# FFN layer pair on one core: first transfer split, thresholds in two steps, and DMA transposes for two operands

## The reference, cut to what matters

```python
x = x + L0_ffn(L0_cond(x, length, conv_w), w_gate, w_up, w_down)
x = x + L1_ffn(L1_cond(x, ...), W_base, ...)        # x: (8, 128, 512)

# L0_cond: y = masked mean of x over its last axis; a 5-tap convolution over the rows; x * sigmoid(.)
# L0_ffn: rows of x rounded to 8-bit integers by their own maximum, weights to -1, 0, 1 by their mean;
#         h = silu(xq @ Wg.T) * (xq @ Wu.T)         # 1376 columns
#         h rounded to integers again, @ Wd.T
# L1_cond: lora_delta = lora_B @ lora_A * 0.5
cb = codebook / max(abs(codebook))
wg = (weight + lora_delta).reshape(512, 4, 128)
normalized = wg / exp(scale_log)
idx = searchsorted((cb[:-1] + cb[1:]) * 0.5, normalized)
w_eff = (cb[idx] * scale).reshape(512, 512) + lora_delta
# x @ w_eff.T, then L1_ffn: x @ W_base.T + b_base + four experts of rank 8 weighted by a softmax
```

## Time and profile before

| | us |
|---|---|
| timed runs | 154.81, 155.97, 156.15 (median 155.97) |
| profiled execution, its own time | 154.66 |
| its span, first to last instruction | 152.9 |
| granted TensorE clock, mean | 1.000 of full speed |

### The profile page before, as it was taken

One profiled execution on the slowest core, in us unless ns is written; L12 is line 12 of the kernel. 1 busy time (PEld: TensorE's weight loads), 2 busy tenths in 40 slices (PEclk: granted clock), 3 DMA queues, 4 the chain that ended last, 5 costly groups with the idle time before them and its releaser, 6 DMA issues.

```text
span 152.9 us, 2333 instructions
## 1 busy us (share of the span) xinstructions
PE 141.7 (93%) x758; PEld 89.2 (58%) x758; DVE 113.8 (74%) x302; ACT 95.8 (63%) x163; POOL 11.0 (7%) x31
## 2 busy tenths in 40 slices
PE   6679999998799959999988999999999999999993
PEld 2256665753356736637636465565576766787792
DVE  2799999989999999999999767979893031035561
ACT  3899998996997966955827479786731403400200
POOL 7000000000000034100005200000000000000000
PEclk9999999999999999999999999999999999999999
DMA  5999999749500000000000000000000000000193
GB/s 166 389 406 417 417 419 399 272 154 392 194 0 0 0 2 4 0 0 0 4 0 0 0 0 6 0 0 2 0 4 0 0 0 0 0 4 0 61 373 115
DMA packets 6687, 16.06 MB, mean 105 GB/s; under 512 B 674, under 2 KB 1058, under 8 KB 6676
## 3 DMA queue, kind: packets, MB, share of 16 engines
q1 hardware_dynamic: 6676, 15.92, 27.5%
HBM read 13.82 MB, written 2.10 MB: 104 GB/s over the span
## 4 chain that ended last, share of the span: by engine, by line
PE 48%; DVE 29%; ACT 10%; issue 8%; DMA 2%; SPq 0%; ACTq 0%
PE bank L924 15%; PE bank L871 9%; ACT tern_d L491 6%; PE bank L837 6%; PE bank L843 6%; DVE hmax L1273 5%; DVE raw_gate L1270 5%; DVE junk L1109 2%; DMA cond<-in_cond_w 2%; DVE rmax L1159 2%; PE bank L882 2%; PE bank L856 2%; ACT cond L457 1%; PE bank L931 1%; DVE tern_i L1154 1%
## 5 line engine op out<-in xcount | busy, mean ns | idle before, releaser
L837 PE MATMUL bank<-tern_g,head_sb 128*128 128x464 bf16 (+1 forms) x96 | 22.5, 357 | 2.0 <-ACT head_sb L528 1.2
L843 PE MATMUL bank<-tern_u,head_sb 128*128 128x464 bf16 (+1 forms) x96 | 22.5, 357 | 0.0
L924 PE MATMUL bank<-m_h,fr 128*128 128x512 f32 (+1 forms) x72 | 22.3, 378 | 0.0
L871 PE MATMUL bank<-tern_d,delta 128*128 128x512 bf16 (+1 forms) x88 | 20.5, 379 | 0.3 <-ACT b_full L666 0.2
L592 ACT ACTIVATE raw_gate<-raw_gate,hq 128x1376 int16<-128x1376 f32 x8 | 11.5, 1440 | 13.0 <-DVE hq L1280 13.0
L1270 DVE TENSOR_TENSOR raw_gate<-bank,wbt 128x464 f32<-128x464 f32 (+1 forms) x24 | 15.1, 631 | 4.5 <-ACT wbt L585 4.4
L585 ACT ACTIVATE wbt<-bank,s_g 128x464 f32<-128x464 f32 (+1 forms) x24 | 15.3, 639 | 1.9 <-PE bank L837 1.9
L1273 DVE TENSOR_REDUCE hmax<-raw_gate 128x1 f32<-128x464 f32 (+1 forms) x24 | 15.1, 630 | 0.8
L750 PE MATMUL bank<-wbt,cond 128*128 128x512 f32 x32 | 14.8, 599 | 0.0
L843 PEld LDWEIGHTS bank<-tern_u,head_sb 128*128 128x128 bf16 x96 | 9.3, 98 | 9.2 <-DVE raw_gate L1270 0.2
L924 PEld LDWEIGHTS bank<-m_h,fr 128*128 128x128 f32 x72 | 13.2, 189 | 2.7
(11 more groups left out here) (174 smaller groups left out, 234.7 us busy)
## 6 DMA issues: line engine op xcount, KB each, us to landing
raw_gate<-in_w_gate_t SPq DMA_DIRECT2D x4, 688.0 KB, 7.6
raw_up<-in_w_up_t SPq DMA_DIRECT2D x4, 688.0 KB, 12.6
xs<-in_x SPq DMA_DIRECT2D x8, 256.0 KB, 13.0
out_x<-xs SPq DMA_DIRECT2D x7, 256.0 KB, 2.2
raw_down<-in_w_down_t SPq DMA_DIRECT2D x2, 768.0 KB, 5.4
cond<-in_cond_w SPq DMA_DIRECT2D x4, 256.0 KB, 4.4
wbt<-in_w_base_t SPq DMA_DIRECT2D x4, 256.0 KB, 9.6
raw_down<-in_w_down_t SPq DMA_DIRECT2D x2, 512.0 KB, 7.6
```

The costliest lines, as they stand in the source:

```text
L837: mm = pe.matmul(bank_g[n % 2][:, 0:w], xq_t[:, b % 2, k, :], tern_g[:, k, f0:f0 + w], start=(k == 0), stop=(k == KH - 1))
L843: mm = pe.matmul(bank_u[n % 2][:, 0:w], xq_t[:, b % 2, k, :], tern_u[:, k, f0:f0 + w], start=(k == 0), stop=(k == KH - 1))
L871: mm = pe.matmul(bank_down[:], h_t[0:rows, b % 2, j, :], tern_d[0:rows, j, :], start=(j == 0), stop=(j == KF - 1))
L924: pe.matmul(bank_y[n_res][:, h0:h1], a[:, b, k, :], m[:, k, h0:h1], start=(n == 0), stop=False)
```

## The change

- The head transfer is split: first the 128 short rows (codebook, lengths, indices, scales; 36 floats each), then LoRA A and B once, as a transfer `lora0` of 64 rows by 1024 floats. The deltas are multiplied from 64 rows, and all four come at the start, after 5 warm-up matmuls instead of 7.
- `scaled_weight(1)` goes from ACT to POOL, as one multiplication of 128x512; `condn_done` becomes one semaphore per quarter, and `normalise(0)` waits slice by slice.
- The thresholds are ordered in two steps: two instructions ahead of `normalise(0)`, four after the second mask.
- Hidden activations 0 to 6 are transposed by one DMA each on SP's queue, from `h_i` (now 1408 columns wide) into one buffer `ht_i`; ACT copies them to `h_t` in two instructions at the end of iteration b+1, right ahead of `hidden_round(b+1)`. Only entry 7 goes through PE.
- Quantised x(3) to x(7) are transposed by DMA on the same queue, two buffers, x(b+3) issued behind h(b). x(0) to x(2) go through PE.
- Order: `x1_transposes(b-3)`, `x1_high` and `x1_low` come after the second chunk, not before it; `fold(3,3)` before `gate_up(0,1)`; m copies in the order 1, 0, 2, 3; `x_max(5, 8)` ahead of `residual(0)`, and the gates and scales of x(5) to x(7) ahead of `x1_low(0)` and `residual(1)`; `conv(2)` right after `gate_up(3,1)`.

```diff
-            sp.dma_start(head_sb[:], head).then_inc(ld_head, 16)
+            sp.dma_start(head_sb[:, 2 * H:HEAD], head).then_inc(ld_head, 16)
+            sp.dma_start(head_sb[0:RANK0, 0:2 * H], lora0).then_inc(ld_lora, 16)
             for k in range(KH):
-                sp.dma_start(cond[:, k, :], cond_v[:, k, :]).then_inc(ld_cond[k], 16)
+                load_cond(k)
...
+            def transpose_x(b):
+                sp.wait_ge(xq_pool_done, b - 1)
+                if b - 2 >= X_BY_DMA:
+                    sp.wait_ge(xt_done, b - 1)
+                sp.dma_start(xt_i[:, b % 2, :, :], xq_bits[:, b % 2, :].bitcast(I16), transpose=True)\
+                    .then_inc(xt_landed[b % 2], 16)
+
+            def transpose_h(b):
+                sp.wait_ge(hint_done, b + 1)
+                if b >= 1:
+                    sp.wait_ge(ht_done, ht_copies(b - 1))
+                sp.dma_start(ht_i, h_i[:, b % 2, :], transpose=True).then_inc(ht_landed, 16)
+
+            for b in range(NB):
+                if b < H_BY_DMA:
+                    transpose_h(b)
+                if X_BY_DMA <= b + 3 < NB:
+                    transpose_x(b + 3)
...
+            for k in SCALED_BY_POOL:
+                pool.wait_ge(inv_done, 1)
+                pool.wait_ge(ld_cond[k], 16)
+                pool.tensor_tensor(cond[:, k, :].rearrange("p (g i) -> p g i", g=KH),
...
-            for n, i in enumerate(T_ORDER):
+            for i in T_ORDER:
                 diagonals(i)
-                if n == 3:
-                    scaled_weight(1)
...
             def hidden_evacuate(b):
+                if b < H_BY_DMA:
+                    act.wait_ge(ht_landed, 16 * (b + 1))
+                    if b >= 2:
+                        act.wait_ge(down_ps, b - 1)
+                    act.activation(h_t[0:FL, b % 2, KW, :], ht_i[0:FL, KW, :], ACT.Copy).then_inc(ht_done, 1)
+                    act.activation(h_t[:, b % 2, 0:KW, :], ht_i[:, 0:KW, :], ACT.Copy).then_inc(ht_done, 1)
+                    return
...
+                if 1 <= b < NB:
+                    hidden_evacuate(b - 1)
                 if b < NB:
                     hidden_round(b)
...
-            pe.wait_ge(ld_head, 16)
-            lora_delta(0)
-            lora_delta(1)
+            pe.wait_ge(ld_lora, 16)
+            for k in range(KH):
+                lora_delta(k)
...
+                gate_up(b, 1)
+                if b == 3:
+                    conv(2)
                 if b >= 4:
                     x1_transposes(b - 3)
-                gate_up(b, 1)
                 if b == 0:
-                    fold(KH - 1, 3)
                     conv(1)
...
-                if b >= 1:
+                if b - 1 >= H_BY_DMA:
                     hidden_transposes(b - 1)
-                if 2 <= b < NB - 1 or b == 0:
+                if b != 1 and b + 1 < X_BY_DMA:
                     x_transposes(b + 1)
...
+            def inner_thresholds():
                 dve.tensor_tensor(t(1), t(1), t(3), ALU.min)
-                link(dve.tensor_tensor(t(5), t(5), t(3), ALU.max))
+                dve.tensor_tensor(t(5), t(5), t(3), ALU.max).then_inc(th_done, 1)
+
+            def outer_thresholds():
+                dve.wait_ge(th_done, 1)
                 dve.tensor_tensor(t(0), t(0), t(1), ALU.min)
...
+            inner_thresholds()
             normalise(0)
-            masks(0, 0, 1)
-            ordered_thresholds()
-            masks(0, 1)
+            masks(0, 0, 2)
+            outer_thresholds()
+            masks(0, 2, 3)
+            dve.wait_ge(th_done, 2)
+            masks(0, 3)
...
                 if b == 3:
+                    x_max(5, NB)
                     residual(0)
+                if b < NB:
+                    hidden_chunk(b, 1)
                 if b >= 4:
                     x1_low(b - 3)
-                if b < NB:
-                    hidden_chunk(b, 1)
...
                 if b == 3:
+                    y_reciprocal(2)
+                    gates(2)
+                    x_scales(5, NB)
                     x1_low(0)
                 if 3 <= b <= NB + 1:
                     residual(b - 2)
```

More of the change, by code:

```diff
@@ L59 @@
 EPS = 1e-5
-WARM_HEAD = 7
+WARM_HEAD = 5
 HALF = TAPS // 2
@@ L63 @@
 GROUPS = [(0, 2), (2, 5), (5, NB)]
-CONV_WITH_XT = {4: 2}
+X_BY_DMA = 3
+H_BY_DMA = 7
+KW = KF - 1
 TINY_SQUARE = 1e-36
 STAND_IN = 1e-15
+SCALED_BY_POOL = (1,)
+M_ORDER = (1, 0, 2, 3)
 T_ORDER = (3, 1, 5, 0, 2, 4, 6)
@@ L75, with build @@
 SUMMED_BY_ACT = 3
-def build(nc, x, head, w_gate_t, w_up_t, w_down_t, cond_w, w_base_t, b_base,
+def build(nc, x, head, lora0, w_gate_t, w_up_t, w_down_t, cond_w, w_base_t, b_base,
           lora1, router, conv_band, out):
@@ L271, in build @@
         delta_ps = sem("delta_ps")
-        condn_done = sem("condn_done")
+        condn_done = [sem(f"condn_done{k}") for k in range(KH)]
         norm_done = sem("norm_done")
@@ L345, in chunk_no, with xt_landings, ht_copies @@
             return NC * b + c
+        def xt_landings(b):
+            return sum(1 for i in range(X_BY_DMA, b + 1) if i % 2 == b % 2)
+        def ht_copies(b):
+            return 2 * min(b + 1, H_BY_DMA) + 3 * max(0, b + 1 - H_BY_DMA)
         block = ctx.enter_context(nc.Block())
@@ L456, in scaled_weight @@
                     c = slice(g * GROUP, (g + 1) * GROUP)
-                    ins = act.activation(cond[:, k, c], cond[:, k, c], ACT.Copy, scale=scl_inv[:, k, g:g + 1])
-                ins.then_inc(condn_done, 1)
+                    act.activation(cond[:, k, c], cond[:, k, c], ACT.Copy,
+                                   scale=scl_inv[:, k, g:g + 1]).then_inc(condn_done[k], 1)
             scaled_weight(0)
@@ L524, in x_evacuate @@
             def x_evacuate(b):
-                act.wait_ge(xt_ps, b + 1)
+                if b < X_BY_DMA:
+                    act.wait_ge(xt_ps, b + 1)
+                    src = bank_xTi[b].rearrange("p (k e) -> p k e", k=KH)
+                else:
+                    act.wait_ge(xt_landed[b % 2], 16 * xt_landings(b))
+                    src = xt_i[:, b % 2, :, :]
                 if b >= 2:
                     act.wait_ge(gu_ps, NC * (b - 1))
-                act.activation(xq_t[:, b % 2, :, :], bank_xTi[b].rearrange("p (k e) -> p k e", k=KH),
-                               ACT.Copy).then_inc(xt_done, 1)
+                act.activation(xq_t[:, b % 2, :, :], src, ACT.Copy).then_inc(xt_done, 1)
             def conv_out(g):
@@ L543, in m_copy @@
                 act.wait_ge(fold_ps, k + 1)
-                if k == 0:
+                if k == M_ORDER[0]:
                     act.wait_ge(tern_out, 2 * NC - 1)
@@ L627, in _ @@
                     silu_chunk(b, 1)
+                if b >= 4:
+                    x1_high(b - 3)
                 if b == 0:
-                    for k in range(KH):
+                    for k in M_ORDER:
                         m_copy(k)
@@ L939, in _ @@
                 gate_up(b, 0)
+                if b == 0:
+                    fold(KH - 1, 3)
                 if b == 1:
@@ L1324, in _ @@
                                       ms_h.bitcast(F32), ALU.subtract).then_inc(msl_done, 1)
-                    x_max(5, NB)
                     y_safe(2)
```

81 lines of the change are left out of this document (44 added, 37 removed).

## The result

The change makes the kernel slightly slower: 157.40 us median (156.58 to 158.03, 10 runs) against 155.95 (154.68 to 156.20, 10 runs) of the kernel before, ratio 1.0115 with a 95% interval of 1.0077 to 1.0154. The forecast was 150.6. The profiled execution has a span of 154.9 us, where before had 152.9.

What follows compares the result with a forecast made beforehand. Bound by hops between engines to about 33 us, DVE to 80.7, then PE; gains of 1.8 us (start) and 2.95 us (loop), together 4.8, took 155.4 to 150.6 us, with an 8-in-10 range of 148.5 to 156.0.

Steps and rivals of the forecast that it cites:

- in the new place PE is idle: Start, PE: two of four deltas leave the place between codebooks 0 and 1, where four took 1.88 us, for idle time.
- The LoRA rows land on 64 partitions at half the rate: Start: the rows land 0.65 us later; with POOL disturbing DVE, the reason for the start gain's lower bound of 1.0 us.
- the 4.65: Start, DVE: `normalise(0)` follows `cond` slice by slice and starts at about 4.65 us instead of 6.26.
- The forecast of 1.8 us for the start: Common gain of the ACT, DVE and PE queues at the start: 1.8 us, bounds 1.0 and 2.2.
- T: Loop: time for a DMA-transposed h to land, taken as 4.5 us, bounds 2.6 and 8.9; up to 4.4 fully hidden.
- x1 transposes 0.44, `down(1)` 2.38: Loop, iteration 3, PE: durations in us summed from 76.75, with two `gate_up` groups of 1.56 each, to 82.7.
- The 0.93 us wait for `residual(1)`: Loop, PE: this wait goes, since the residual is ready at 82.05 and PE arrives at 82.7.
- 1.1 us lost to the later start: Loop: loss from the later `x1_transposes(0)`, in the count that was to agree with the loop's 2.95 us gain.
- A: Rival: the transposed transfer becomes the loop's bound, from T = 6.2 us; at T = 7, 159.5 us; chance 0.18.
- B: Rival: half the gain, T between 5 and 6 us; 152.7 to 153.5 us at 5.5; chance 0.16.
- D: Rival: silu and products arrive late each turn, 0.4 us a turn for four turns; 152.2 us; chance 0.14.
- C: Rival: the start gives 0.8 us instead of 1.8, loop as forecast; 151.6 us; chance 0.10.

Runs made afterwards that it cites:

- `warm11`: The changed kernel with 11 warm-up matmuls instead of 5; 153.71 us, ratio 0.990 against the kernel before.
- `rows128`: The changed kernel, 5 warm-ups kept, with the deltas read from 128 rows, the lower 64 set to zero by POOL; 153.80 us, ratio 0.993 against before.
- `both_fixed`: `lora128` plus the 12 extra matmuls of `filler` ahead of `x1_transposes(0)`; 151.85 us, ratio 0.978 against the kernel before.
- `lora128`: The changed kernel with the LoRA rows doubled to 512 KB on 128 partitions and 9 warm-ups; 153.01 us, ratio 0.984 against the kernel before.
- `filler`: The changed kernel with 11 warm-ups and 12 unread matmuls in the wait ahead of `x1_transposes(0)`; 152.04 us, ratio 0.979 against the kernel before.
- `loop_only`: The change's loop alone (DMA transposes, their copies, new order) with the old start; 153.87 us, ratio 0.9917 against the kernel before.
- `down_first`: The changed kernel with 11 warm-ups and `down(1)` ahead of `x1_transposes(0)` on PE; 153.70 us, ratio 0.987 against the kernel before.
- `xmax_late`: The changed kernel with 11 warm-ups and `x_max(5, 8)` back behind the subtraction of `ms` on DVE; 153.26 us, ratio 0.987 against the kernel before.
- `start_only`: The change's start alone, 5 warm-ups included, with the old loop; 158.93 us, ratio 1.0234 against the kernel before.

## Why the prediction was wrong

**The step that failed first: "in the new place PE is idle".** That the place was free was true; the price of what moved there was taken at full clock without a look at what PE did before. The change also cuts the warm-ups from 7 to 5, and this was not priced at all. The warm-ups end at 3.5 us, 1.54 us before the LoRA rows land, and the deltas then run at 0.85 us a record where the forecast had 0.47: about 3 us more for eight, and `codebook(0)`'s first matmuls at 0.43 apart come on top. `warm11` and `rows128` leave the rest as it is and bring the first product 3.7 (2.6 to 3.1 in three later profiles) and 2.0 us forward; with `both_fixed` it is 4.0 (44.81 to 40.80), of the 4.8 us by which the start missed. The other 0.8 is the forecast's 1.8 against a true 1.0, next.

**"The LoRA rows land on 64 partitions at half the rate"** stood as a mere lower bound. The runs bear it out: 3.8 us for 256 KB in the change and for 512 KB in `lora128`. The rows landed at 5.0 us, which the prediction itself had named as a sign that it is wrong at the start (later than 4.5). The Trainium skill (SBUF — State Buffer, Door 1: The DMA port swizzle) says that partitions 0 to 63 reach only 8 of 16 DMA ports; this case's landing times agree in the ratio. `cond(0)`, queued behind it, was scaled 0.74 us later than before where 0.65 earlier was forecast, and 0.62 of that is the extra issue on SP's queue, a term that the sum did not have; in `lora128`, with all partitions, it is no earlier. And `normalise(0)` needs delta(0) as well as `cond(0)`, which the 4.65 left out: even in `both_fixed`, at full clock, it waits for PE and starts at 6.18, 1.23 us behind the first delta and 0.08 ahead of before. The forecast of 1.8 us for the start came out, with the clock put right, at 1.0 (41.81 to 40.80), its own lower bound: 0.45 to 0.7 from the deltas' place, the rest from thresholds, POOL and head together, which no run parts further and which one profile each can barely tell from nothing. POOL's scaling took 1.04 us, within what was allowed.

**The loop: right mechanism, one term mis-sized.** Right were the iteration of 7.47 us (7.46 measured), T within its bounds and in the median below the 4.5 taken (3.5; for x 2.7 against 2.8), and `x1_transposes(0)` later by about what `x_max` costs (forecast 1.54 us behind its old place; 35.18 us behind the first product instead of 33.40, so 1.8). The mis-sized term is "x1 transposes 0.44, `down(1)` 2.38": the wait that the reordering makes lets the clock fall, and the two took 4.54 us in place of 3.00. `filler` makes the loop 1.39 us shorter than after (69.23 to 67.84), and 1.53 shorter than `warm11`, of the 2.0 us missed.

Of the other 0.6, 0.24 is the later start of `x1_transposes(0)`. The 0.93 us wait for `residual(1)` is gone, but only just: the forecast had the residual ready 0.65 us ahead of PE, in `filler` PE is there first and loses about 0.1 us at 83.52. And 0.16 was never time: the sum starts from the timeline's 75.21 and is held against the 112.34 of the earlier trace rows, and there the same group of PE stands 0.16 us later than in the timeline (85.28 against 85.12). About 0.1 was not traced. The "1.1 us lost to the later start" isn't derived either, its own sum has 1.54; it was counted as a wait only, and the text never asked what PE does after standing still for 2.6 us.

**The rivals.** A and B (T above 5 or 6.2 us) fell: 3.5 us in the median, 5.0 once, and ACT's waits for landed h, 2.08 us at most, never reached PE. D fell too: the iterations are PE's own work. C was the nearest, "the start gives little", but as a gain of 0.8, not a loss of 3.0. No rival and no bound had the clock in it, and that is why the range of 148.5 to 156.0 missed the 157.4.

## What to carry to other kernels

When work moves on TensorE, or a wait is added ahead of it, ask first what the engine did before: price it at both levels of the clock, not at the mean of old rows, and look at the distance between starts, since the granted clock may print 1.00 beside matmuls at half speed. A wait of PE is best closed at its cause; where DVE's list only moves it elsewhere, matmuls that nobody reads can hold the clock in a wait that is there anyway, and here they were worth 1.5 us. A transfer that is split also costs its issue: every load behind it goes out later (0.6 us here). Count a changed number of warm-ups as a part of the change like any other, and let them end when the first operand lands, neither earlier nor later.

## What was not expected of the hardware

- Eight float32 matmuls on 64 rows, 7.19 us without a gap, left the clock at its lower level (0.85 us a record) in two kernels; on 128 rows, the lower 64 of them zeros, the clock rose during the seventh of the same eight (6.62 us) in one. Once it was up, 64 rows kept it (3.70 us).
- A wait of 2.62 us dropped it in the profiles of all five kernels that have it unfilled (after, `loop_only`, `warm11`, `rows128`, `lora128`: granted clock 0.57 to 0.67 over the 4 us behind it, `down(1)` at 3.7 to 4.2 us instead of 2.5); waits of 1.60 and 1.72 us between full matmuls, in `down_first` and `xmax_late`, did not. The Trainium skill (TensorE: Matmul & The Clock Gate, Loop structure matters more than you think) sets a loop in which every matmul waits long for a DMA, and PE goes cold, against one in which DVE copies the result out and the next matmuls follow immediately. Here they did not follow immediately, since PE had to wait for DVE, and the clock fell: it is the wait that counts, whoever is waited for.
- The mean granted clock of an execution is no measure of what the clock cost. Three of the four executions of `lora128` list 1.000 and take 152.75 to 153.23 us, the profiled one 0.989 and 153.06. In the kernel before, 1.000 and 0.989 part the executions cleanly, by about 1 us.
- There is a second dip in the profile of the kernel after, at 59 to 63 us, and some 4 us earlier in `warm11` and `both_fixed`, and in none of the others. It follows a wait of 1.66 us for POOL and then matmuls on 16 rows; the groups there take 1.7 us instead of 0.95. It costs nothing in these kernels, since DVE leads there: the loops of `warm11` and `lora128` are 69.37 and 69.38 us, with and without it. The same instructions thus drop the clock in one kernel's execution and not in another's (`lora128` and `rows128` have the same wait and no dip), and a wait of 1.66 us is no safe one.
- The moment at which the clock rises at the start differs between executions: 14.9 us after, 17.4 us in `start_only`, with the same instructions on PE; the same 11 warm-ups took 4.22 or 4.88 us. Differences under 1 us between starts mean little in a single profile.
- A DMA transpose of 128x1408 two-byte elements inside SBUF lands 3.5 us after its issue (5.0 when queued behind another), 128x512 after 2.7, far nearer to the stores of the earlier trace rows than to 1408 single pieces, though the packets of queue 1 rose from 6676 to 19556.
